# Two stages of a graph network on one core: own tiles, earlier loads and another order at the seam between the stages

## The chip, the core and the metric

The kernel runs on one core of a Trainium2 chip: TensorE (PE) for matmuls, with its weight loads shown apart (PEld), VectorE (DVE), ScalarE (ACT), GpSimd (POOL), and SyncE (SP), which here only issues DMAs. The engines work side by side and hand over by semaphores. The metric is the device time in microseconds (us); lower is better. The kernel before takes 1154.79 us (median of 3 runs, 1154.49 to 1154.93).

## What is computed

3125 nodes with 256 features, 53125 edges sorted by target node. Cut to what matters (`seg` is the segment sum over target nodes):

```
n   = seg(w * x[src])                                   # stage 1
o   = leaky(x @ W1.T + b1 + (n + n*x) @ W2.T + b2)
x1  = layernorm(x + o / |o|)
e   = relu(edge_attr @ ee_w1 + ee_b1) @ ee_w2 + ee_b2   # edge network
h   = (1+eps)*x1 + seg(x1[src] + e)                     # stage 2
h   = relu(ln(h @ w1 + b1)); h = relu(ln(h @ w2 + b2))  # 256 -> 1024 -> 1024
y   = relu(ln(x1 + h @ w3 + b3))
out = layernorm(x1 + y)
```

## The kernel before

Nodes are tiled in 25 blocks of 128 rows, edges in 17 tiles of 128 per block (the last block, number 24, has 8). Every fp32 operand of a large product is split in a high part (rounded to the PE's fast format) and a low part (the rest), and the products high-high, high-low and low-high are summed in PSUM.

**Stage 1**, blocks 0 to 24. POOL gathers the 17 tiles `raw` of source rows, ACT and DVE make from them the messages `msg` (high, low), DVE makes one-hot matrices `oh` from the targets, PE sums messages per target (`ps_sum`, `near_step`), and also runs the edge network's first layer (`ps_e`). A block's tail follows one and two blocks later, interleaved: `take_s` (DVE, makes `s_r` from the sum and the node rows `xs`), `turn` (PE transposes), `turned` (ACT, `sT`), `products` (PE, into `ps_d` and, for the edge part, `ps_w` or `ps_e`), `leak`, `norm`, `deviation`, `table_high` (ACT), and eleven DVE steps `tail(b, 1)` to `tail(b, 11)`: step 1 makes `o`, 4 reads the node rows again (`xr`), 6 aggregates the statistics, 8 makes x1, 9 makes `tb`, 10 the low half of the block's `table` (x1 plus the edge bias, in two halves), 11 makes `hb`. SP stores `table`, x1 and `hb` to HBM (`store_table`, `put_table`, `store_hb`). `table`, `x1` and `hb` have two tiles each, used in turn, so `hb` of block 24 may only be written when the store of `hb` of block 22 has landed. Block 24 already has its own tile for x1 and table.

**Stage 2**, 25 iterations p: first block 24 (p = 0), then block 0, 1, ... . POOL gathers `table` rows from HBM into `grow` (256 KB a tile), PE sums them by one-hots into `ps_s`, DVE makes `h` (`take_h`), PE transposes it (`turn_h`), ACT and DVE split it (`h_high`, `h_low`), then come `layer1`, `layer2`, `layer3` on PE with `stats`, `scalars`, `normalize` (`zn`), PE transposes (`turn_z`), `relu` on ACT and `split` on DVE between them. From p = 2 on the iterations run in one steady order; p = 0 and p = 1 (`first_block`, `late_iteration`) are written apart.

**The seam.** Rows of the last four blocks are not in HBM when the first gathers of stage 2 run. So the early gathers fetch zero rows for them, and `add_absent` adds their share by PE from count matrices `counts` and the table tiles on chip. Block 21's table tile has been reused by then: SP loads it back from HBM (`far_row`). The weights of stage 2 (`w_raw`) are split at the seam too: ACT makes the high parts (`weight_highs(first, end)`, one 128x1024 instruction per piece, 12 pieces), PE copies a high half into a PSUM bank (`copy_highs`, a matmul with the identity `ident_r`), DVE subtracts it from the raw weights (`first_lows`, `weight_lows_from_copies`). Semaphores `w_high`, `w_copied`, `w_ready` count these; `half_bank(m)` says which PSUM bank copy m uses, and `half_bank_free(m)` how many lows must be done before.

The order of the work is written out by hand in each engine's program: an instruction waits until its semaphores stand, and everything behind it on its engine waits with it. SP issues its DMAs in program order as well.

## Time and profile before

| | |
|---|---|
| median of 3 runs | 1154.79 us |
| the profiled execution | 1154.48 us, its span 1152.7 us |
| granted clock of PE over the span | 0.990 |
| stage 1, a block | about 21.3 us |
| PE busy | 95% of the span |
| DVE / ACT / POOL busy | 85% / 58% / 69% |

The page of the profile gives busy shares, 40 slices of the span and the costliest groups. The seam lies at about 526 to 590 us. There the timeline of each engine (start, duration, line, operation, what was written from what, and in brackets the idle time before it with what ended it) and tables by stretches of time are the views to read. Matmul durations in the timeline contain a pipeline latency; the distance between starts is the pace.

### The profile page before, as it was taken

How to read it: one execution, taken by the hardware profiler on the slowest of the kernel's cores; microseconds unless marked ns; L12 is line 12 of the kernel's file. 1: busy time of each engine (PE TensorE's matmuls, PEld its weight loads, DVE VectorE, ACT ScalarE, POOL GpSimd, SP SyncE). 2: the span in 40 equal slices, each digit the busy share in tenths (PEclk: the TensorE clock that was granted, in tenths of full speed). 3: DMA queues.
4: the chain of work that ended last, by engine and by line, in shares of the span. 5: the costliest groups of instructions: out<-in, count | busy, mean ns of one | idle time of the engine just before them, and what ended most of it. 6: DMA issues, size and time to landing. Idle time of an engine off the chain costs nothing.

```text
span 1152.7 us, 21077 instructions
## 1 busy us (share of the span) xinstructions
PE 1095.8 (95%) x5335; PEld 905.8 (79%) x5335; DVE 975.2 (85%) x2792; ACT 663.5 (58%) x1600; POOL 800.0 (69%) x840
## 2 busy tenths in 40 slices
PE   6899999999999999998789999999999999999996
PEld 4688778787787787776578888888888888888885
DVE  7899999999999999998688778877887788778865
ACT  4576777776767776666434454445444544454453
POOL 7777777777777777777567767767776777677610
PEclk9899999999999999999899999999999999999999
DMA  8457667677676566668767777777777777777720
GB/s 228 135 159 202 196 198 209 190 202 207 185 207 182 167 177 178 175 175 267 215 186 221 217 204 215 216 207 211 208 216 207 211 208 215 208 210 208 205 72 12
DMA packets 105664, 222.26 MB, mean 193 GB/s; under 512 B 19959, under 2 KB 56689, under 8 KB 105586
## 3 DMA queue, kind: packets, MB, share of 16 engines
q0 software_dynamic: 53408, 164.16, 50.9%
q1 hardware_dynamic: 52178, 57.25, 16.1%
q8 instruction: 27, 0.44, 0.2%
q14 instruction: 51, 0.42, 0.1%
HBM read 203.97 MB, written 17.36 MB: 192 GB/s over the span
## 4 chain that ended last, share of the span: by engine, by line
PE 52%; POOL 20%; issue 16%; DVE 6%; DMA 4%; ACT 1%; POOLq 0%; SPq 0%; DVEq 0%; ACTq 0%
PE ps_z L1251 29%; POOL raw L873 20%; PE ps_s L1206 9%; PE ps_y L1251 6%; PE ps_tr L1320 3%; DMA raw<-in_x,src_all 3%; DVE oh L158 1%; DVE msg L1966 1%; DVE msg L1972 1%; DMA hbase_dram<-hb 1%; PE ps_e L1005 1%; POOL raw L858 1%; DMA xr<-in_x 1%; PE ps_tr L1245 1%; PE ps_sum L1010 0%
## 5 line engine op out<-in xcount | busy, mean ns | idle before, releaser
L928 POOL DMA_INDIRECT grow<-table_dram,src_all x401 | 386.3, 963 | 166.0 <-issue 96.9
L873 POOL DMA_INDIRECT raw<-in_x,src_all x399 | 378.9, 950 | 121.6 <-issue 113.0
L1251 PE MATMUL ps_z<-w_high,a 128*128 128x512 f32 x784 | 252.9, 394 | 0.5 <-DVE a L2296 0.5
L1005 PE MATMUL ps_e<-we,attr 65*128 65x256 f32 x832 | 224.8, 391 | 15.7 <-DVE msg L1972 13.5
L158 DVE TENSOR_SCALAR oh<-lane,rel 128x128 fp32r<-128x128 f32 x919 | 221.1, 300 | 18.3 <-DMA raw<-in_x,src_all 18.2
L1010 PE MATMUL ps_sum<-msg,oh 128*128 128x512 f32 x464 | 227.6, 491 | 7.3 <-DVE msg L1972 7.3
L1524 ACT ACTIVATE msg<-raw,w_sb 128x256 fp32r<-128x256 f32 x416 | 193.9, 500 | 64.3 <-DMA raw<-in_x,src_all 54.2
L1005 PEld LDWEIGHTS ps_e<-we,attr 65*128 65x128 f32 x832 | 154.0, 194 | 55.0 <-issue 32.3
L1966 DVE SCALAR_TENSOR_TENSOR msg<-raw,w_sb,msg 128x256 fp32r<-128x256 f32 x416 | 181.7, 473 | 6.6 <-ACT msg L1527 6.6
L1012 PE MATMUL ps_sum<-msg,oh 128*128 128x512 f32 x464 | 183.9, 396 | 0.0
L1251 PEld LDWEIGHTS ps_z<-w_high,a 128*128 128x128 f32 x784 | 147.3, 188 | 30.8 <-issue 0.9
L1707 ACT ACTIVATE aF<-ps_tr,be,g 128x128 f32<-128x128 f32 x392 | 144.2, 464 | 37.9 <-PE ps_tr L1320 37.9
L1251 PE MATMUL ps_z<-w_low,a 128*128 128x512 f32 x392 | 152.9, 390 | 0.0
L1972 DVE SCALAR_TENSOR_TENSOR msg<-ps_e,msg 128x512 fp32r<-128x512 f32 (+1 forms) x220 | 142.6, 648 | 0.0
L1527 ACT ACTIVATE msg<-ps_e 128x512 fp32r<-128x512 f32 (+1 forms) x220 | 122.5, 557 | 14.3 <-PE ps_e L1005 14.1
L1206 PE MATMUL ps_s<-grow,oh 128*128 128x512 f32 x455 | 120.1, 400 | 2.4 <-DVE oh L158 2.4
L1010 PEld LDWEIGHTS ps_sum<-msg,oh 128*128 128x128 f32 x464 | 88.3, 190 | 32.1 <-issue 15.8
L2251 DVE BATCH_NORM_STATS2 bs<-ps_z 128x6 f32<-128x512 f32 x100 | 69.6, 697 | 44.7 <-PE ps_z L1251 44.6
L1012 PEld LDWEIGHTS ps_sum<-msg,oh 128*128 128x128 f32 x464 | 88.9, 192 | 15.7
L1206 PEld LDWEIGHTS ps_s<-grow,oh 128*128 128x128 f32 x455 | 83.6, 188 | 18.8 <-DVE oh L158 3.2
L1713 ACT ACTIVATE fm<-fm,ln_eps 128x1 f32<-128x1 f32 x50 | 14.7, 295 | 129.7 <-DVE fm L2256 129.7
L1251 PE MATMUL ps_y<-w_high,a 128*128 128x256 f32 x400 | 83.4, 292 | 2.5 <-DVE a L2309 2.1
(168 smaller groups left out, 1500.5 us busy)
## 6 DMA issues: line engine op xcount, KB each, us to landing
attr<-in_attrT SPq DMA_DIRECT2D x50, 192.0 KB, 4.5
raw<-in_x,src_all POOLq DMA_INDIRECT x416, 3.0
grow<-table_dram,src_all POOLq DMA_INDIRECT x401, 3.7
table_dram<-table SPq DMA_DIRECT2D x24, 256.0 KB, 2.8
w_raw<-in_m_w SPq DMA_DIRECT2D x48, 128.0 KB
attr<-in_attrT SPq DMA_DIRECT2D x24, 160.0 KB, 4.2
xs<-in_x SPq DMA_DIRECT2D x25, 128.0 KB
xTb<-in_xT SPq DMA_DIRECT2D x25, 128.0 KB
```

What stands on the lines that cost most here:

```text
L158: ins = dve.tensor_scalar(out_[:, i, :], lanes, which[:, i:i + 1], None, ALU.is_equal)
L873: pool.indirect_dma_start(out=raw[:, j, :], out_offset=None, in_=x, in_offset=bass.IndirectOffsetOnAxis(ap=src_all[:, q * TILES + j:q * TI ...
L928: pool.indirect_dma_start(out=grow[:, j, :].bitcast(F32), out_offset=None, in_=table_dram, in_offset=bass.IndirectOffsetOnAxis(ap=src_all[ ...
L1005: mm = pe.matmul(ps_e[k % 3][:, (j - j0) * D:(j - j0 + 1) * D], attr[:, j * P:(j + 1) * P], we1[:, :], start=True, stop=True)
L1010: pe.matmul(ps_sum[bank][:, :], oh[:, slot, :], msg[:, j, 0, :], start=start, stop=False, skip_group_check=True)
L1012: return pe.matmul(ps_sum[bank][:, :], oh[:, slot, :], msg[:, j, 1, :], start=False, stop=stop, skip_group_check=True)
L1206: return pe.matmul(ps_s[:, :], oh[:, slot, :], grow[:, j, :], start=start, stop=stop, skip_group_check=True)
L1251: mm = pe.matmul(acc, left[a], right[b], start=False, stop=stop and a == 1, skip_group_check=True)
L1524: act.activation(msg[:, j, 0, 0:D], raw[:, j, :], ACT.Copy, scale=w_sb[:, tile_cols(n, j)])
L1707: ins = act.activation(aF[layer][:, k, :], ps_tr[:, half, c * P:(c + 1) * P], ACT.Relu, bias=bb[:, k:k + 1], scale=gg[:, k:k + 1])
L1966: dve.scalar_tensor_tensor(msg[:, j, 1, 0:D], raw[:, j, :], w_sb[:, tile_cols(n, j)], msg[:, j, 0, 0:D].bitcast(F32), ALU.mult, ALU.subtract)
L1972: dve.scalar_tensor_tensor(msg[:, j0:j0 + m, 1, D:2 * D], ps_e[k % 3][:, 0:m * D].rearrange("p (j d) -> p j d", d=D), 0.0, msg[:, j0:j0 + ...
```

## The change

- `own_table`: block 23 gets an own table tile too, so block 21's stays on chip in `table[1]`, and the load of `far_row` goes.
- `hb` of block 24 is written to a free tile (`raw[:, 1, :]`), is not stored to HBM, and its wait on the store of block 22 goes.
- The last rows of x (`xs`, `xT` of block 24, `xr` of block 23) go to free `raw` tiles and are loaded in the middle of block 23, `res` already in block 15.
- The first bias (512 KB) has its own tile and is loaded in block 21 in four parts, the scales `g`, `be` in block 22; `bng`, `bnb` (128 KB each) are loaded after the last stores.
- The one-hots of block 24's steps 2 and 3 are made by ACT, inside block 23 (`last_one_hots`: per step two squares of 128x128 and one relu of 128x256), no longer by DVE.
- Tails of the last three blocks on DVE, `weight_highs` on ACT, `copy_highs` and the sums of p = 1 on PE are reordered; copies 12 to 19 use four banks, not two.

```diff
             def table_at(b, par):
-                return last_table if is_last(b) else table[par]
+                return own_table[b] if isinstance(b, int) and b in own_table else table[par]
+            def hb_at(b, par):
+                return raw[:, 1, :] if is_last(b) else hb[par]
...
-            last_table = w3_high[:, 1:3, :]
-            far_row = w3_high[:, 3:5, :].rearrange("p a d -> p (a d)")
+            own_table = {BLOCKS - 1: w3_high[:, 1:3, :], BLOCKS - 2: w3_high[:, 3:5, :]}
...
             def half_bank(m):
...
-                return (ps_y[:, :], ps_z[1][:, 1, :] if m < FIRST_HALVES else ps_tr[:, 1, :])[m % 2]
+                if m < FIRST_HALVES:
+                    return (ps_y[:, :], ps_z[1][:, 1, :])[m % 2]
+                return (ps_z[0][:, 0, :], ps_z[0][:, 1, :], ps_y[:, :], ps_tr[:, 1, :])[(m - FIRST_HALVES) % 4]
...
             def half_bank_free(m):
...
-                return 5 if m == 8 else m - 1
+                if m < FIRST_HALVES:
+                    return 5 if m == 8 else m - 1
+                if m < FIRST_HALVES + 4:
+                    return FIRST_HALVES - 1 if m == FIRST_HALVES + 2 else 0
+                return m - 3
...
             def load_weight_part(b, part):
...
+                if b == FIRST_COUNT + TILES + 2:
+                    sp.wait_ge(counted, TILES)
+                    sp.dma_start(bias_0[:, cols], m_b1[:, cols]).then_inc(bias_in[0], 16)
...
                 for b in range(1, BLOCKS - 1):
...
                    load_xT(b)
                    load_weight_part(b, 2)
+                    if b == BLOCKS - 2:
+                        sp.wait_ge(message, NP * b + 6)
+                        sp.dma_start(xT_at(b + 1), xT[:, :, bass.ds((b + 1) * P, P)]).then_inc(late_xT_in, 16)
+                        sp.dma_start(xs_at(b + 1), rows(x, b + 1)).then_inc(late_xs_in, 16)
+                        sp.dma_start(xr_at(b), rows(x, b)).then_inc(late_xr_in[0], 16)
...
-                sp.dma_start(res[:, :], rows(x, BLOCKS - 1)).then_inc(xr_last_in, 16)
-                load_xs(BLOCKS - 1)
-                load_xT(BLOCKS - 1)
-                load_xr(BLOCKS - 2)
-                sp.wait_ge(counted, TILES)
-                load_consts()
-                sp.wait_ge(message, NP * (BLOCKS - 1) + LAST_PAIRS)
-                sp.wait_ge(table_stored, 16 * (BLOCKS - ABSENT_BLOCKS + 1))
-                sp.dma_start(far_row.bitcast(F32), rows(table_dram, BLOCKS - ABSENT_BLOCKS)).then_inc(row_in, 16)
-                load_bias(0)
                 store_table(BLOCKS - 3, 0)
                 store_hb(BLOCKS - 3, 0)
                 store_table(BLOCKS - 2, 1)
                 put_table(BLOCKS - 1, 0)
                 load_bias(1)
                 store_hb(BLOCKS - 2, 1)
-                store_hb(BLOCKS - 1, 0)
+                load_norms()
...
+            def last_one_hots(path, c):
+                last, n = BLOCKS - 1, c - LAST_OH
+                span, j0, m = path.steps[c]
+                lanes = lane[:, (1 - span) * P:(2 - span) * P]
+                wait(act, last_oh, n)
+                for j in range(m):
+                    at = last * TILES + j0 + j
+                    act.activation(sq[:, j * P:(j + 1) * P], lanes, ACT.Square, bias=rel_columns[:, at:at + 1],
+                                   scale=-1.0).then_inc(last_squared, 1)
+                act.wait_ge(last_squared, m * (n + 1))
+                act.wait_ge(summed, SUMS * (last - 1) + c + 1)
+                act.activation(oh[:, path.slot[c]:path.slot[c] + m, :].rearrange("p j n -> p (j n)"), sq[:, 0:m * P],
+                               ACT.Relu, bias=ones_c[:, :], scale=-1.0).then_inc(last_oh, 1)
...
                 def first_block():
-                    h_high(0)
-                    act.wait_ge(bias_in[0], 16)
+                    act.wait_ge(bias_in[0], 64)
                     act.wait_ge(w_ready, 1)
                     open_z(0, 0, 0)
                     act.wait_ge(w_ready, 2)
                     open_z(0, 0, 1)
-                    weight_highs(5, 8)
+                    h_high(0)
+                    weight_highs(4, KD + KH - 2)
...
                 def first_block(path):
...
                     add_absent(1)
-                    sums(path, 1, 1, SPLIT_SUM)
-                    copy_highs(FIRST_HALVES, FIRST_HALVES + 2)
+                    sums(path, 1, 1, 2)
+                    copy_highs(FIRST_HALVES, FIRST_HALVES + 4)
                     layer2_with(0, 0, w2_high, 0, KH // 2)
-                    copy_highs(FIRST_HALVES + 2, FIRST_HALVES + 3)
+                    copy_highs(FIRST_HALVES + 4, FIRST_HALVES + 5)
                     layer2_with(0, 0, w2_high, KH // 2, KH)
-                    copy_highs(FIRST_HALVES + 3, FIRST_HALVES + 4)
+                    copy_highs(FIRST_HALVES + 5, FIRST_HALVES + 6)
+                    sums(path, 1, 2, LAST_PAIRS)
```

DVE at the end of stage 1 and the start of stage 2, before: `hb` of block 24 (which waits for a store), four one-hots, then `h` (p = 0).

```order
L2140 TENSOR_TENSOR w_low<-w_raw,ps_z 128x512 [waits w_copied]
L2030 TENSOR_TENSOR w_high<-tb,w_high 128x256 [waits da_end2]
L2036 SCALAR_TENSOR_TENSOR hb<-raw,eps_t,ps_e 128x256 [waits hb_stored,edge_dense,dd_end2]
L158 TENSOR_SCALAR oh<-lane,rel 128x128 [waits sum_done]
L158 TENSOR_SCALAR oh<-lane,rel 128x128 x3
L2238 TENSOR_TENSOR h<-ps_s,hb 128x256 [waits dd_end2,absent_added,sum_done]
```

The same place of DVE now.

```order
L2197 TENSOR_TENSOR w_low<-w_raw,ps_z 128x512 [waits w_copied]
L2086 TENSOR_TENSOR w_high<-tb,w_high 128x256 [waits da_end2]
L2093 SCALAR_TENSOR_TENSOR raw<-raw,eps_t,ps_e 128x256 [waits edge_dense,dd_end2]
L2197 TENSOR_TENSOR w_low<-w_raw,ps_z 128x512 [waits w_copied]
L2294 TENSOR_TENSOR h<-ps_s,raw 128x256 [waits dd_end2,absent_added,sum_done]
```

The wait `hb_stored` is gone, the second weight low stands behind `hb`, and the four one-hots have moved behind the first `stats` of p = 0.

ACT from the message of block 24's tiles 6 and 7 to x1's deviation of block 23, before (`sT` are the transposes of block 23, then of block 24).

```order
L1623 ACTIVATE ident_r<-ident 128x128 [waits counted]
L1534 ACTIVATE sT<-ps_t 128x512 [waits edge_dense,s_turned]
L1516 ACTIVATE w_high<-w_raw 128x1024 [waits edge_net,w_in]
L1551 ACTIVATE st<-st,ln_eps 128x1 [waits dd_end0]
L1539 ACTIVATE ol<-ps_d 128x256 [waits dd_end0,dense]
L1545 ACTIVATE sq,st<-o 128x256 [waits dd_end1]
L1547 ACTIVATE st<-st 128x1 [waits da_end1]
L1555 ACTIVATE table<-tb 128x256 [waits dd_end0]
L1516 ACTIVATE w_high<-w_raw 128x1024
L1534 ACTIVATE sT<-ps_t 128x512 [waits edge_dense,s_turned]
```

And now.

```order
L1677 ACTIVATE ident_r<-ident 128x128 [waits message]
L1570 ACTIVATE sT<-ps_t 128x512 [waits edge_dense,s_turned]
L1552 ACTIVATE w_high<-w_raw 128x1024 [waits edge_net,w_in]
L1552 ACTIVATE w_high<-w_raw 128x1024
L1587 ACTIVATE st<-st,ln_eps 128x1 [waits dd_end0]
L1575 ACTIVATE ol<-ps_d 128x256 [waits dd_end0,dense]
L1581 ACTIVATE sq,st<-o 128x256 [waits dd_end1]
L1583 ACTIVATE st<-st 128x1 [waits da_end1]
L1570 ACTIVATE sT<-ps_t 128x512 [waits edge_dense,s_turned]
L1591 ACTIVATE table<-tb 128x256 [waits dd_end0]
```

Both first weight highs stand ahead of block 23's `leak` (`ol`), and block 24's `sT` ahead of block 22's `table` high.

PE around the start of the second layer of p = 0, before (`a` is the split result of the first layer; the copies are those from the identity).

```order
L1206 MATMUL ps_s<-grow,oh 128x512 [waits got4,oh2_ready]
L1206 MATMUL ps_s<-grow,oh 128x512 [waits got5]
L1193 MATMUL ps_y<-w_high,ident_r 128x512 [waits w_ready,w_high]
L1193 MATMUL ps_tr<-w_high,ident_r 128x512 [waits relu_out0,w_ready,w_high]
L1287 MATMUL ps_z<-w_high,a 128x512 [waits a_ready0,z_open1_0]
L1287 MATMUL ps_z<-w_high,a 128x512 x7
L1193 MATMUL ps_y<-w_high,ident_r 128x512 [waits w_ready,w_high]
L1287 MATMUL ps_z<-w_high,a 128x512 [waits a_ready0]
L1287 MATMUL ps_z<-w_high,a 128x512 x7
L1193 MATMUL ps_tr<-w_high,ident_r 128x512 [waits w_ready,w_high]
```

And now.

```order
L1230 MATMUL ps_z<-w_high,ident_r 128x512 [waits w_high] x2
L1230 MATMUL ps_y<-w_high,ident_r 128x512 [waits w_ready,w_high]
L1230 MATMUL ps_tr<-w_high,ident_r 128x512 [waits relu_out0,w_high]
L1324 MATMUL ps_z<-w_high,a 128x512 [waits a_ready0,z_open1_0]
L1324 MATMUL ps_z<-w_high,a 128x512 x7
L1230 MATMUL ps_z<-w_high,ident_r 128x512 [waits w_ready,w_high]
L1324 MATMUL ps_z<-w_high,a 128x512 [waits a_ready0]
L1324 MATMUL ps_z<-w_high,a 128x512 x7
L1230 MATMUL ps_z<-w_high,ident_r 128x512 [waits w_ready,w_high]
L1243 MATMUL ps_s<-grow,oh 128x512 [waits got4,oh2_ready]
```

The second layer now starts behind step 1 of p = 1 and four copies, not behind steps 1 and 2 and two copies, and the sums 2 and 3 stand later.

## Rows read from the trace of the kernel before

**Rows 1.** The page, part 1: busy time and share of the span.

```profile
PE 1095.8 (95%) x5335; PEld 905.8 (79%) x5335; DVE 975.2 (85%) x2792; ACT 663.5 (58%) x1600; POOL 800.0 (69%) x840
```

**Rows 2.** Table by stretches: length, busy (instructions) by engine, clock, DMA share, GB/s.

```profile
540.00:560.00 20.00, 13.83 (x62) 10.49 (x60) 12.88 (x33) 9.77 (x18) 10.49 (x12) 0.83 0.90 314
600.00:620.00 20.00, 20.00 (x96) 16.56 (x95) 14.37 (x48) 6.24 (x17) 15.12 (x17) 1.00 0.76 226
```

**Rows 3.** Timeline of PE at the seam: start, duration, what, idle before it.

```profile
551.53 1.22 PE L1193 MATMUL ps_z<-w_high,ident_r 128*128 128x512 f32 x2 [4.18 <-DVE hb L2036]
...
568.94 0.73 PE L1206 MATMUL ps_s<-grow,oh 128*128 128x512 f32 x2 [2.14 <-DVE oh L158]
...
569.97 3.38 PE L1287 MATMUL ps_z<-w_high,a 128*128 128x512 f32 x8
...
573.57 2.07 PE L1287 MATMUL ps_z<-w_high,a 128*128 128x512 f32 x8
...
581.05 0.40 PE L1251 MATMUL ps_z<-w_high,a 128*128 128x512 f32 x1
...
590.68 1.07 PE L1320 MATMUL ps_tr<-ident,zn 128*128 128x128 f32 x8
```

**Rows 4.** Timeline of DVE at the seam.

```profile
551.00 0.48 DVE L2036 SCALAR_TENSOR_TENSOR hb<-raw,eps_t,ps_e 128x256 f32<-128x256 f32 x1 [4.21 <-DMA hbase_dram<-hb]
551.39 0.87 DVE L158 TENSOR_SCALAR oh<-lane,rel 128x128 fp32r<-128x128 f32 x4
552.18 0.42 DVE L2238 TENSOR_TENSOR h<-ps_s,hb 128x256 f32<-128x256 f32 x1
552.51 0.68 DVE L2214 TENSOR_TENSOR w_low<-w_raw,ps_z 128x512 fp32r<-128x512 f32 x1
...
560.31 0.81 DVE L2276 TENSOR_SCALAR zn<-ps_z,mv 128x512 f32<-128x512 f32 x1
...
567.94 1.06 DVE L158 TENSOR_SCALAR oh<-lane,rel 128x128 fp32r<-128x128 f32 x5
...
579.12 0.42 DVE L2240 TENSOR_TENSOR h<-ps_s,hbx 128x256 f32<-128x256 f32 x1 [1.37 <-PE ps_s L1206]
...
587.41 1.28 DVE L2251 BATCH_NORM_STATS2 bs<-ps_z 128x6 f32<-128x512 f32 x2
```

**Rows 5.** The chain that ended last: start, duration, what.

```profile
540.42 10.45 DMA hbase_dram<-hb
```

**Rows 6.** Timeline of SP at the seam.

```profile
536.62 0.43 SPq L707 DMA_DIRECT2D bias<-in_m_b  x1
...
537.63 0.34 SPq L665 DMA_DIRECT2D table_dram<-table  x1
...
550.71 0.38 SPq L665 DMA_DIRECT2D table_dram<-w_high  x1
```

**Rows 7.** Waits of SP, 500 to 600 us: total, times, longest.

```profile
SPq L657 <- DMA table_dram<-table: 7.5, 1, 7.5
```

**Rows 8.** Groups by line and form, ACT: busy, mean ns.

```profile
L1516 ACT ACTIVATE w_high<-w_raw 128x1024 fp32r<-128x1024 f32 x12 | 12.2, 1052 | 0.0
...
L1575 ACT ACTIVATE squares<-lane,rel 128x128 f32<-128x128 f32 x17 | 6.7, 395 | 0.0
```

**Rows 9.** Table by stretches, PE only: busy (instructions), clock, DMA share, GB/s.

```profile
550.00:551.00 1.00, 0.00 (x0) 0.50 0.40 151
556.00:557.00 1.00, 1.00 (x5) 0.70 0.76 201
```

**Rows 10.** The same table as rows 9, in stage 1.

```profile
130.00:151.00 21.00, 20.18 (x94) 1.00 0.70 199
469.00:490.00 21.00, 20.18 (x90) 1.00 0.62 176
```

**Rows 11.** Timeline of POOL at the seam.

```profile
553.72 0.94 POOL L928 DMA_INDIRECT grow<-table_dram,src_all  x1 [6.47 <-DMA table_dram<-w_high]
```

**Rows 12.** The page, part 6: a DMA issue, count, KB, median us to landing.

```profile
table_dram<-table SPq DMA_DIRECT2D x24, 256.0 KB, 2.8
```

167 lines of the change are left out of this document (96 added, 71 removed).

## The prediction

> **What bounds the kernel now.** I read the page first, then a table by stretches, then the timelines of PE, DVE, ACT, SP and POOL at the seam, and last the chain that ended last. PE is busy for 1095.8 of 1152.7 us [rows 1]. In the steady part of stage 2 it is busy 20.00 of 20 us; at the seam 13.83 of 20 us, at a mean granted clock of 0.83 [rows 2]. So stage 2 is bound by PE, and whatever brings PE earlier into its steady order is gained in full; the change can pay only at the seam. PE's timeline there shows the holes: 4.18 us before 551.53 that DVE's `hb` ended, 2.14 us before 568.94 that a one-hot ended, and between them the first layer-2 half of p = 0 at 569.97 took 3.38 us where the same 8 matmuls took 2.07 us at 573.57 [rows 3]. The next iteration's layer 2 begins at 581.05, and the transposes that need `zn` of iteration 1 at 590.68 [rows 3]. DVE's timeline names the cause of the first hole: `hb` of block 24 at 551.00 after 4.21 us idle, ended by the store of `hb` of block 22 [rows 4]; the chain shows that store from 540.42 on, 10.45 us [rows 5].
>
> Why it takes so long: SP had just issued four loads of rows, four small ones, `bng`, `bnb`, `far_row` and, at 536.62, a 512 KB bias, then at 537.63 the store of block 22's table [rows 6], whose landing SP itself awaited for 7.5 us [rows 7]. The table of block 24 was issued at 550.71 only [rows 6].
>
> **The change part by part.** I carry each engine's order of the changed kernel forward by the durations of the rows, from 529 us on; up to there I expect nothing.
>
> *Term 1, up to `h` of p = 0 (DVE, 552.18 before).* The wait of 4.21 us goes, since the new tile waits for no store. The four one-hots between `hb` and `h`, 551.39 to 552.18, move behind `h`: 0.8 us. The loads of `xs`, `xT`, `xr` are issued in block 23, some 12 us earlier; the idle 0.55 us of DVE for `xs` at 536.47, 1.35 us of PE for `xT` and 0.85 us of DVE for `xr` go, and DVE is rid of the last four one-hots of stage 1, another 0.8 us. Against that, two weight highs, not one, now stand on ACT ahead of block 23's `leak`; one costs 1.05 us, so 0.95 us later by start to start [rows 8]; and one weight low (0.68 us long, 0.6 in a row [rows 4]) stands where DVE was idle before. Of about 2.2 us gained and 1.5 us lost here I keep 0.6. Sum 5.6 us: `h` at about 546.6. Bounds: 4.2 us (inputs help nothing) to 6.5 us (the highs find a gap).
>
> *Term 2, from `h` to the start of layer 2 (552.18 to 569.97 before, 17.8 us).* PE's granted clock was 0.50 at 550 to 551 and only back within 556 to 557 [rows 9]: it fell inside the hole before 551.53, so the 12 matmuls of layer 1 ran at 1.2 GHz. Without that hole I expect 2.4 GHz, and DVE's idle time for `stats`, about 1.9 us, goes; the moved one-hots come in, 0.8 us. From `zn` (560.31) on, DVE's list is the same work with one more low in it, 0.6 us, which stood before it earlier. So the splits of p = 0 end about 14.8 us after `h`, before 15.8. And layer 2 starts with the first half of the split, not after the one-hots that ended at 569.0 (five, 1.06 us at 567.94 [rows 4]), two sums and two copies: that is 1.0 us before the end of the splits, where it was 2.0 us behind it. Term 2: 1.0 + 3.0 = 4.0 us. Layer 2 at about 560.4, 9.6 us sooner.
>
> *Term 3, from there to iteration 1 (569.97 to 581.05 before, 11.1 us).* 48 matmuls and sums at 0.23 us are left, at full clock, plus one wait of about 0.9 us for the low of copy 12, which now stands behind the one-hots: 8.8 us. Gain 2.3 us, of which 1.3 is the clock (3.38 against 2.07 us [rows 3]), the rest the 1.4 us that the copies waited in turn on two banks, now four. PE would be 11.9 us sooner at this point.
>
> *Term 4, given back.* DVE gets `h` of p = 1 at about 569.3, against 579.12, 9.9 us sooner; behind it stand the same lows, two direct lows and one-hots before `stats` at 587.41 [rows 4]. From there to ACT's `zn` is 3.13 us, and PE's transposes at 590.68 had 0.14 us of slack. DVE comes 10 us sooner, PE 11.9: PE waits the difference here. This is the new late one. The gain at 590 is 10.0 us, and in the steady order PE is the bound again.
>
> *Costed at nothing.* Block 24's one-hots on ACT: two squares of 0.395 us [rows 8] and a relu, 1.15 us a step by start to start, 2.3 us in block 23. They lie in ACT's idle time before block 21's `tb` (1.95 us) and ahead of message 2, which DVE wants 0.7 us later than it would now be ready. If that cover is gone it costs up to 1 us. The 512 KB of bias in block 21, with 128 KB of `res` in block 15: blocks with 512 KB of weight loads (130 to 151) and without (469 to 490) have the same 20.18 us of PE in 21 [rows 10], so nothing; the queue of SP sees 0.43 us per issue between attribute loads that wait for PE anyway. The three loads in block 23 stand ahead of block 21's store, which waits for DVE until 527.95. POOL's list is unchanged; its first gather of p = 1 waits for block 24's table, at 553.72 before [rows 11]. I expect the table stored from about 545.6 on, and the gather at 548.4; the first four tiles are wanted at 558.8 and land by 557.
>
> For what the stores will take the trace bounds it by 10.45 us [rows 5] and by the 2.8 us that a table store takes in the median [rows 12]; I take 4 us, nearer to the low end, because 5.9 MB are asked of the queues in the 23 us from 526 on, 256 GB/s, where 540 to 560 shows 314 GB/s as its mean [rows 2].
>
> The Trainium skill's page DMA: Bandwidth & Descriptors, section Queues, rings and completion order, says that one issuer's descriptors are consumed in ring order while an engine takes turns between rows. By that rule the store was late mainly because of the 1.5 MB which SP itself had put ahead of it, not because of POOL's gathers, and the late store would vanish with those loads; by a shared limit alone it would shrink less. The 7.5 us which SP waited fits both, and no row here separates them.
>
> The sum: 5.6 + 4.0 + 2.3 - 1.9 = 10.0 us. I take off 0.5 us for some ten handovers between engines which I chained without any slack (estimate, 0.05 us each, as between `hb` and its release). The profiled execution took 1154.48 us, its span 1152.7; the median of the runs is 0.3 us above it. 1154.5 - 9.5 = 1145.0 us.
>
> **The rivals.**
>
> *A, the clock or a hole stays.* PE is still sparse from 543 to 560 by my schedule, somewhat over half busy, with holes of 1 to 2 us. If the clock falls once more, as it did between 568.94 and 573.57 after a hole of 2.14 us, that costs 1.3 to 2.7 us: 1146.5 to 1148. For it: that very fall. Against: 536 to 540 was as sparse, with 1.35 us of hole, and kept its clock.
>
> *B, the stores stay slow.* If block 24's table still goes out at 550.7, the tiles of p = 1 land 3.3 us after they are wanted, and layer 2 shifts by as much: 1148.3. For it: the DMA engines are 0.90 busy in 540 to 560 [rows 2], and the gathers, most of that, remain. Against: a quarter of the bytes of that stretch are gone.
>
> *C, only the wait goes.* If the reordered tails and highs do nothing, 4.2 us of `hb`, 0.8 us of one-hots and the clock at 2.7 us are left, minus 1 us given back: about 6.7 us, 1147.8; 1150 if the clock stays as well.
>
> *D, slower.* One mechanism: PE's clock falls before `h` and stays at 1.2 GHz until layer 2 of p = 1, because the change spreads PE's work more thinly (copies one by one, each behind a low of DVE). From copy 4 to there some 76 matmuls of 128x512 would take 0.2 us more each, 15 us, against 10 gained: 1159.6. It decides from about 50 slow matmuls on. Against: before, the clock came back after 5 us of work which was no denser.
>
> *E, the tiles don't free anything*, because another wait of the same kind (x1 of block 23 on the store of block 21) ends as late: same as before. Against: that x1 came at 540.46 with no idle time.
>
> **How the numbers follow.** My forecast, 1143 to 1146.5: 0.54. A 0.2, B 0.09, C 0.09, D 0.03, E 0.02, faster than 1143 (term 4 is not taken, up to 12 us gained, or 6.5 in term 1) 0.03. The range 1141.8 to 1149.5 leaves out D, E, the worse end of C and some of the unforeseen. 0.2% is 2.3 us, about what a measurement of this kernel can tell from no change: faster 0.95, same 0.02, slower 0.03.
>
> **What would show it.** Right: no idle time on DVE before `hb` of block 24, `h` of p = 0 near 546.6, the granted clock at 1.00 from 546 to 557, layer 2 of p = 0 near 560.4, iteration 1's layer 2 near 569, the table of block 24 issued before 547, and a wait of PE of about 1.5 us at the transposes near 579 to 581. Wrong: a clock of 0.50 anywhere from 546 to 580 (A, D), POOL's first gather of p = 1 later than 551 (B), `leak` of block 23 on ACT over 1 us later than before (C), or more than 0.5 us idle on DVE in block 23 before the messages (the one-hots on ACT are not covered).

## The result

The changed kernel takes 1145.99 us (median of 6 runs, 1145.09 to 1147.71) against 1154.84 us of the kernel before (median of 6, 1154.37 to 1155.55) in the same comparison: ratio 0.9926, 95% interval 0.9916 to 0.9937, so 8.9 us less. Predicted were 1145.0 us, 1141.8 to 1149.5. The profiled execution took 1146.01 us, its span is 1144.2 us, its mean granted clock 0.992. Medians here and below are of all executions of a kernel, ratios of the undisturbed (fast) ones only, so the two need not divide evenly (in e9 above all).

### The profile after

The page, part 1, which answers to [rows 1]: PE has the same work in 8.5 us less span.

```profile
PE 1094.9 (96%) x5335; PEld 905.1 (79%) x5335; DVE 974.2 (85%) x2788; ACT 666.5 (58%) x1606; POOL 799.4 (70%) x840
```

The table by stretches, columns as in [rows 2]: PE is busy for 16.46 us of the seam's 20, not 13.83, but at the same mean clock of 0.83. The stretch from 600 on, which was full, now has a hole of 0.28 us.

```profile
540.00:560.00 20.00, 16.46 (x71) 12.20 (x70) 17.10 (x47) 15.27 (x28) 10.68 (x11) 0.83 0.85 270
600.00:620.00 20.00, 19.72 (x106) 16.55 (x105) 14.24 (x38) 10.25 (x25) 15.13 (x17) 1.00 0.75 218
```

DVE's timeline, which answers to [rows 4]: `hb` of block 24 (now written to `raw`) has no idle time, and `h` of p = 0 comes at 545.98. `stats` still waits 0.70 us for PE.

```profile
544.99 0.47 DVE L2093 SCALAR_TENSOR_TENSOR raw<-raw,eps_t,ps_e 128x256 f32<-128x256 f32 x1
545.98 0.41 DVE L2294 TENSOR_TENSOR h<-ps_s,raw 128x256 f32<-128x256 f32 x1
550.51 0.70 DVE L2307 BATCH_NORM_STATS2 bs<-ps_z 128x6 f32<-128x512 f32 x1 [0.70 <-PE ps_z L1288]
570.64 0.42 DVE L2296 TENSOR_TENSOR h<-ps_s,hbx 128x256 f32<-128x256 f32 x1 [3.96 <-PE ps_s L1243]
```

PE's timeline, which answers to [rows 3]: the copies no longer stand behind a hole of 4.18 us but of 1.50 us, layer 2 of p = 0 begins at 562.55, that of p = 1 at 570.44, and the transposes of p = 1 now wait 1.51 us for `zn`. At 612.06 PE waits for a gathered tile.

```profile
545.13 0.50 PE L1217 MATMUL ps_s<-w_high,counts 128*128 128x256 f32 x2 [1.50 <-DVE w_high L2086]
546.45 0.69 PE L1282 MATMUL ps_tr<-ident,h 128*128 128x128 f32 x2 [0.20 <-DVE h L2294]
...
554.78 1.07 PE L1357 MATMUL ps_tr<-ident,zn 128*128 128x128 f32 x8 [1.36 <-ACT zn L1748]
557.37 2.07 PE L1243 MATMUL ps_s<-grow,oh 128*128 128x512 f32 x4 [0.19 <-DVE oh L159]
562.55 1.97 PE L1324 MATMUL ps_z<-w_high,a 128*128 128x512 f32 x8
570.44 0.39 PE L1288 MATMUL ps_z<-w_high,a 128*128 128x512 f32 x1
581.85 1.07 PE L1357 MATMUL ps_tr<-ident,zn 128*128 128x128 f32 x8 [1.51 <-ACT zn L1748]
612.06 0.50 PE L1243 MATMUL ps_s<-grow,oh 128*128 128x512 f32 x1 [0.24 <-DMA grow<-table_dram,src_all]
```

The same stretches for PE alone (busy, clock, DMA share, GB/s), as [rows 9]: the clock fell twice. The four sums at 557.37, for example, took 2.07 us; e6 below, whose clock was up there, took 1.19.

```profile
546.00:550.00 4.00, 3.68 (x11) 0.57 0.89 266
550.00:556.00 6.00, 4.60 (x25) 1.00 0.80 269
556.00:560.00 4.00, 3.68 (x8) 0.57 0.82 241
560.00:576.00 16.00, 16.00 (x71) 1.00 0.76 224
```

SP's and POOL's timelines, which answer to [rows 6, 11]: block 24's table goes out at 546.37, not at 550.71, and yet POOL's first gather of p = 1, which waits for it, starts at the same time as before.

```profile
538.97 0.33 SPq L700 DMA_DIRECT2D table_dram<-table  x1
...
546.37 0.41 SPq L700 DMA_DIRECT2D table_dram<-w_high  x1
```

```profile
553.75 0.94 POOL L963 DMA_INDIRECT grow<-table_dram,src_all  x1 [6.29 <-DMA table_dram<-w_high]
```

The DMA view (KB each, us from issue to landing) of block 22's table store, first in the kernel before (issued at 537.63 [rows 6]), then in the changed one (538.97):

```profile
table_dram<-table SPq DMA_DIRECT2D x1, 256.0 KB, 10.6
```

```profile
table_dram<-table SPq DMA_DIRECT2D x1, 256.0 KB, 3.7
```

I follow the lead over the kernel before at PE's transposes of `h`, one per iteration: 6.20 us at p = 0 (552.65 to 546.45), 10.63 at p = 1, 8.76 at p = 2, 8.20 at p = 3, and from there to the end a slow rise to 8.62. So the seam decides, and what the lead is at p = 3 is what the kernel gains. The table shows it for all profiled executions that can be compared.

| kernel | p = 0 | 1 | 2 | 3 | median us | ratio to before (95%) |
|---|---|---|---|---|---|---|
| changed | 6.20 | 10.63 | 8.76 | 8.20 | 1145.99 | 0.9926 (0.9916 to 0.9937) |
| e1, own `hb` tile alone | 4.70 | 6.03 | 4.52 | 4.52 | 1150.05 | 0.9967 (0.9954 to 0.9980) |
| e2, `hb` wait back | 5.35 | 9.49 | 7.60 | 7.61 | 1146.65 | 0.9936 (0.9922 to 0.9950) |
| e3, holes filled | 6.19 | 12.18 | 10.55 | 8.87 | 1144.24 | 0.9913 (0.9898 to 0.9928) |
| e4, fillers in the kernel before | -1.75 | -0.45 | -0.44 | -0.43 | 1154.26 | 0.9998 (0.9989 to 1.0007) |
| e5, one-hots on DVE | 6.21 | 10.52 | 8.76 | 8.78 | 1145.92 | 0.9931 (0.9917 to 0.9945) |
| e6, old PE order | 5.55 | 7.64 | 6.12 | 6.12 | 1148.38 | 0.9952 (0.9938 to 0.9966) |
| e7, old ACT order | 5.56 | 9.50 | 6.32 | 6.34 | 1146.23 | 0.9925 (0.9913 to 0.9938) |
| e8, loads late | 2.00 | 7.95 | 6.17 | 6.17 | 1147.33 | 0.9934 (0.9920 to 0.9948) |

The kernel before took 1153.89 us beside e1 to e4 and 1154.99 us beside e5 to e8, so medians of different groups compare only roughly. By the ratios e6 is 3.0 us slower than the changed kernel (2.4 by the medians), e2 1.2, e8 0.9, e5 0.6, e7 0.1 faster and e3 1.5 faster; of these only e6 has an interval that does not overlap that of the changed kernel.

A profiled execution is one of a kernel's runs; where it is not near the median (e7: 1147.64 us, the longest of its six) its leads say how that one went, not what the edit costs. It can also come to the seam late for a reason that lies long before it: DVE's `o` of block 22 stands at 528.10 in the changed kernel and within 0.12 us of it in e1, e2, e3 and e5, but at 528.29 in e7, 528.67 in e8 and 528.76 in e6, and e6 was 0.67 us behind at 121 us already. So 0.66 us of e6's smaller lead, 0.57 of e8's and 0.19 of e7's are not their edits'. And in e1, e6 and e7 the clock fell once more, within 588 to 596 (third layer of p = 1; 0.68 in e6 and 0.57 in e7 at 588 to 592, 0.74 in e1 at 592 to 596), behind the usual waits for `zn`. I read the loss of 1.5 us from p = 1 to p = 2 in e1 and e6, and part of the 3.2 in e7, as that.

### The profile page after: what moved, and what is told of

Read it like the earlier page. It is cut to its first block, busy times and chain, and to the rows that moved or that the text cites. A ratio compares the mean times of both kernels' runs of the same rounds, so it can differ in the third digit from the quotient of the medians.

```text
span 1144.2 us, 21077 instructions
## 1 busy us (share of the span) xinstructions
PE 1094.9 (96%) x5335; PEld 905.1 (79%) x5335; DVE 974.2 (85%) x2788; ACT 666.5 (58%) x1606; POOL 799.4 (70%) x840
## 4 chain that ended last, share of the span: by engine, by line
PE 51%; POOL 20%; issue 17%; DVE 7%; DMA 3%; ACT 1%; SPq 1%; POOLq 0%; DVEq 0%; ACTq 0%
PE ps_z L1288 27%; POOL raw L908 19%; PE ps_s L1243 8%; PE ps_y L1288 6%; PE ps_tr L1357 3%; DMA raw<-in_x,src_all 2%; DVE oh L159 2%; DVE msg L2020 1%; DVE msg L2026 1%; PE ps_e L1040 1%; POOL grow L963 1%; PE ps_sum L1045 1%; PE ps_sum L1047 1%; DMA attr<-in_attrT 1%; PE ps_tr L1282 0%
```

## The experiments

### e1: the own tile of `hb` alone

The kernel before with one part of the change: block 24's `hb` in `raw[:, 1, :]`, not stored, no wait.

```diff
+            def hb_at(b, par):
+                return raw[:, 1, :] if is_last(b) else hb[par]
...
-                    wait(dve, hb_stored, 16 * (b - lag))
+                    if not is_last(b):
+                        wait(dve, hb_stored, 16 * (b - lag))
```

> The kernel before with one edit: hb of block 24 has its own tile, is not stored, and waits for no store. Theory 1 (the wait was one of several causes, and the clock another): hb at about 546.8 us, h of p = 0 at 548, 4.2 us sooner; POOL's first gather of p = 1 still near 553.7, so step 1 of p = 1 waits a little for its tiles; PE's clock still falls once or twice. Time about 1150, 4 to 5.5 us under before. Rival (the wait alone is the gain of the change): 1146 to 1147, within 1 us of the changed kernel.

Measured: 1150.05 us, ratio 0.9967; lead 4.70 us at p = 0 and 4.52 at the end. Theory 1 holds, the rival (the wait alone is the whole gain) falls. The clock stayed up where it had been 0.50 [rows 9], and fell later, at 562 to 568, behind PE's wait of 2.00 us for a one-hot:

```profile
546.00:550.00 4.00, 2.58 (x11) 1.00 0.96 347
550.00:556.00 6.00, 4.66 (x24) 1.00 0.88 266
556.00:562.00 6.00, 4.74 (x20) 1.00 0.79 216
562.00:568.00 6.00, 5.05 (x15) 0.72 0.69 206
```

So the wait of 4.21 us [rows 4] is worth about half of the whole gain, and the clock that it had cost was mostly paid again a little later.

### e2: the wait back in the changed kernel

```diff
             def hb_at(b, par):
-                return raw[:, 1, :] if is_last(b) else hb[par]
+                return hb[par]
...
-                    if not is_last(b):
-                        wait(dve, hb_stored, 16 * (b - lag))
+                    wait(dve, hb_stored, 16 * (b - lag))
```

> The changed kernel, but hb of block 24 is written to the shared tile again and waits for the store of block 22. It tells what made that store slow. Theory 1 (the loads which SP had put ahead of it): the store is issued near 541.3 and lands after some 6 us, so DVE idles about 2 us before hb (not 4.2), and the time is 1147 to 1148.5. Rival (the early gathers alone keep the DMA engines full, the store takes 10 us as before): DVE idles 6 us before hb, near 551.5, and the time is 1151 to 1152.

Measured: 1146.65 us, ratio 0.9936; its interval overlaps that of the changed kernel. DVE's timeline shows the wait, 0.56 us, where theory 1 expected some 2 us and a time of at least 1147:

```profile
545.74 0.48 DVE L2092 SCALAR_TENSOR_TENSOR hb<-raw,eps_t,ps_e 128x256 f32<-128x256 f32 x1 [0.56 <-DMA hbase_dram<-hb]
```

The store was issued at 541.30 and landed 4.4 us later, where it had taken 10.45 us [rows 5]. The rival (still 10 us) falls. The two parts are alternatives: with the loads out of SP's way the new tile saves 0.6 us of waiting, without that 4.2. The Trainium skill's page DMA: Bandwidth & Descriptors, section Queues, rings and completion order, has one issuer's descriptors consumed in ring order on each DMA engine, and the prediction drew from it that the late store would vanish with the 1.5 MB ahead of it; by this rule, the run agrees, with 4.4 for 10.45 us. But it does not single the rule out. The same 1.5 MB are gone from all that is in flight too, and a limit shared by all queues would also make the store faster; how much, no run here shows.

### e3 and e4: work for PE in its holes

Matmuls of 128x512 that nobody reads, into free PSUM banks. In e3 six of them stand in the changed kernel ahead of the last counts (the hole of 1.50 us), five ahead of the transposes at 554.78, two behind a copy, ahead of sums that wait for a one-hot; in e4 seven and seventeen in the two holes of the kernel before.

```diff
+                def fill(bank, m):
+                    for _ in range(m):
+                        pe.matmul(bank, ident_r[:, :], flat(pieces[0][1], 0), start=True, stop=True,
+                                  skip_group_check=True)
...
+                        if p == 0 and n == ABSENT_BLOCKS - 1:
+                            pe.wait_ge(dd_end[-1], 1)
+                            fill(ps_tr[:, 1, :], 6)
```

> The changed kernel with matmuls on PE whose results nobody reads, in the two holes in which its granted clock fell: 6 of 128x512 ahead of block 24's share in the sum of p = 0, 5 ahead of the transposes of the first layer of p = 0, 2 behind copy 10. Theory 1 (what is missing to the forecast is PE's clock at 1.2 GHz from 546 to 550 and from 557 to 560): the clock stays at 1.00 through 546 to 561, layer 2 of p = 0 starts near 560.5 and not 562.5, and the time is 1143.5 to 1144.5. Rival (the clock is off the path, DVE sets the pace there): the clock stays up and the time is the same, 1145.7 to 1146.3; with the fillers in the way, 1146.5.

Measured: 1144.24 us, ratio 0.9913, the fastest kernel here, though its interval overlaps that of the changed one. Theory 1 holds in the trace, the rival (the clock is off the path) does not. The clock stayed up through the seam:

```profile
546.00:550.00 4.00, 3.29 (x15) 1.00 0.98 317
550.00:556.00 6.00, 5.60 (x27) 1.00 0.95 313
556.00:560.00 4.00, 3.99 (x17) 1.00 0.79 226
560.00:576.00 16.00, 15.60 (x69) 1.00 0.74 218
```

PE's timeline has the schedule of the prediction: layer 2 at 560.49 (predicted 560.4), the transposes of p = 1 waiting 1.35 us (1.5), and, behind it, waits for gathered tiles.

```profile
560.49 1.98 PE L1333 MATMUL ps_z<-w_high,a 128*128 128x512 f32 x8
...
580.15 1.06 PE L1366 MATMUL ps_tr<-ident,zn 128*128 128x128 f32 x8 [1.35 <-ACT zn L1759]
...
610.21 0.47 PE L1252 MATMUL ps_s<-grow,oh 128*128 128x512 f32 x1 [0.88 <-DMA grow<-table_dram,src_all]
611.39 0.50 PE L1252 MATMUL ps_s<-grow,oh 128*128 128x512 f32 x1 [0.28 <-DMA grow<-table_dram,src_all]
```

The lead of 10.55 us at p = 2 fell to 8.87 at p = 3. Against e3 the changed kernel is 2.06 us late at layer 2 of p = 0 (562.55 against 560.49), 1.55 at that of p = 1, 1.79 at p = 2: the price of its two falls of the clock. At p = 3 it is 0.67: the kernel that comes sooner loses more to the wait for tiles.

> The kernel before with such matmuls in its hole: 7 ahead of block 24's share, 17 more while PE waits for hb of block 24. It prices the first fall of the clock by itself. Theory 1: the clock stays at 1.00 from 546 to 560, layer 1 of p = 0 takes 2.7 us and not 4, DVE's stats come 1.5 to 2 us sooner, the time is 1152.7 to 1153.5. Rival (DVE has enough other work at that place): the clock stays up, the time is within 0.5 us of before.

Measured: 1154.26 us, ratio 0.9998 (0.9989 to 1.0007). This prices nothing: the clock had fallen ahead of the first fillers (0.60 at 544 to 546), and the seventeen ran on past the `h` for which the hole waited, so PE's transposes of it came at 554.40 instead of 552.65. The filler was too large for the hole it was to fill.

### e5: the last one-hots back on DVE

```diff
-                    if b == BLOCKS - 2 and s in (6, 8):
-                        last_one_hots(path, LAST_OH if s == 6 else LAST_OH + 1)
...
                 take_s(before, SUMS * last, 1)
+                near_oh(path, last, 2)
+                near_oh(path, last, 3)
                 messages(2)
```

> The changed kernel (0.9926 of before, 1145.99 us), with one thing undone: the one-hots of block 24's steps 2 and 3 are made by DVE again, behind the first two messages' place, not by ACT inside block 23. Theory 1 (they were on DVE's path at the end of stage 1, four of 128x128, 0.8 us together): hb of block 24 and h of p = 0 come 0.8 us later (h at about 546.8 instead of 545.98), and the time is 1146.4 to 1146.8 us at the same before, 0.4 to 0.8 more than the changed kernel. Rival (ACT's one-hots only fill a gap which DVE had too, because DVE waits for PE or POOL there): h within 0.2 us of 545.98 and the time within 0.3 us of the changed kernel.

Measured: 1145.92 us, ratio 0.9931, and `h` of p = 0 at 545.97, where the changed kernel has 545.98:

```profile
545.97 0.41 DVE L2290 TENSOR_TENSOR h<-ps_s,raw 128x256 f32<-128x256 f32 x1
```

This execution came to the seam 0.12 us ahead (`o` of block 22 at 527.98), so the four one-hots cost 0.11 us of the 0.8 that theory 1 gave them; the rest is covered by waits of DVE that were there anyway. Theory 1 falls, the rival holds: to move them to ACT brought next to nothing. The run shows something else. SP issued block 24's table at 545.14, 1.23 us sooner, since its own wait for earlier stores was shorter; it landed in 5.4 us, POOL's gathers began at 551.31, and the lead stayed at 8.78 us from p = 2 to 3, where the changed kernel lost 0.56 us. POOL also stood still once, which it did not in the changed kernel:

```profile
551.31 0.98 POOL L963 DMA_INDIRECT grow<-table_dram,src_all  x1 [4.18 <-DMA table_dram<-w_high]
...
568.32 0.95 POOL L963 DMA_INDIRECT grow<-table_dram,src_all  x1 [0.72 <-PE ps_s L1240]
```

### e6: PE's order and banks undone

Copies 12 to 19 on two banks, sums 2 and 3 of p = 1 ahead of the first half of layer 2, ACT's openings of `ps_z` in the old place.

```diff
-                    sums(path, 1, 1, 2)
-                    copy_highs(FIRST_HALVES, FIRST_HALVES + 4)
+                    sums(path, 1, 1, SPLIT_SUM)
+                    copy_highs(FIRST_HALVES, FIRST_HALVES + 2)
```

> The changed kernel with PE's order around layer 2 of p = 0 undone: copies 12 to 19 use two banks again, the sums 2 and 3 of p = 1 stand ahead of the first half, and ACT opens ps_z of the next layer in its old order. Tiles, loads and one-hots stay as changed. Theory 1 (my terms 2 and 3: layer 2 starts 3.0 us sooner relative to DVE's splits, the two banks cost 1.4 us): layer 2 of p = 0 starts at about 565 instead of 562.55, iteration 1's layer 2 at 572.5 to 573.5 instead of 570.44; but the changed kernel gave 1.9 us of PE's lead back to DVE at the transposes near 581.85, so only what exceeds 1.9 us reaches the end, less the second fall of the clock that may go with denser work: 1146.3 to 1147.5 us. Rival (the order costs nothing, since DVE sets the pace up to the transposes at 581.85): h of p = 1 and the transposes at the same times as in the changed kernel, time within 0.3 us of it.

Measured: 1148.38 us, ratio 0.9952, whose interval lies just above that of the changed kernel: 2.4 us more by the medians, and more than the 1147.5 us that theory 1 allowed. PE waits again for the one-hots, starts layer 2 at 564.01 and p = 1 at 573.40, and the transposes of p = 1 wait for nothing:

```profile
562.97 0.73 PE L1237 MATMUL ps_s<-grow,oh 128*128 128x512 f32 x2 [2.66 <-DVE oh L159]
564.01 1.98 PE L1318 MATMUL ps_z<-w_high,a 128*128 128x512 f32 x8
...
573.40 0.39 PE L1282 MATMUL ps_z<-w_high,a 128*128 128x512 f32 x1
...
583.08 1.06 PE L1351 MATMUL ps_tr<-ident,zn 128*128 128x128 f32 x8
```

The clock stayed at 1.00 from 546 to 576, so this execution is best compared with e3, whose clock did too. From PE's transposes of `h` of p = 0 to layer 2 of p = 1, e3 needs 22.4 us (546.46 to 568.89), e6 26.3 us (547.10 to 573.40): the order is worth 3.9 us there. To the transposes of p = 1 e3 needs 33.7 us, e6 36.0: 2.3 us are left, the rest is given back. The medians of e6 and of the changed kernel differ by 2.4, but the clock fell in other places in the two, so that this is nearly the same number proves little. Theory 1 holds for the places and the direction, the rival falls.

### e7: ACT's order of the weight highs undone

```diff
-                weight_highs(0, 2)
+                weight_highs(0, 1)
...
+                weight_highs(1, 2)
                 turned(last)
```

> The changed kernel with ACT's order of weight_highs undone: one high, not two, ahead of block 23's leak, one behind block 23's table high, and in stage 2 the highs 5 to 8 in one piece behind the openings of ps_z. Theory 1 (moving them makes the early copies and lows ready sooner, and the last lows do not wait for ACT behind h): hb of block 24 comes up to 0.9 us sooner since leak is not delayed, but the highs behind h are late and DVE or PE waits for w_ready after it: together 1145.8 to 1147.5 us. Rival (the two highs ahead of leak are a pure delay of 0.95 us and the rest is covered): hb at 544.0 to 544.4 instead of 544.99, and 1145.0 to 1145.5 us.

Measured: 1146.23 us, ratio 0.9925: no difference by the medians. But its profiled execution has `hb` of block 24 at 545.63, 0.64 us later than the changed kernel, not sooner; it was 0.16 us behind before (`o` of block 23 at 535.49, not 535.33), so the edit's share is about 0.5. ACT's timelines say why, first that of e7, then that of the changed kernel:

```profile
535.01 0.38 ACT L1575 ACTIVATE ol<-ps_d 128x256 f32<-128x256 f32 x1 [0.81 <-PE ps_d L1109]
...
537.25 1.04 ACT L1552 ACTIVATE w_high<-w_raw 128x1024 fp32r<-128x1024 f32 x1
538.20 0.58 ACT L1570 ACTIVATE sT<-ps_t 128x512 f32<-128x512 f32 x1
```

```profile
532.62 2.00 ACT L1552 ACTIVATE w_high<-w_raw 128x1024 fp32r<-128x1024 f32 x2
534.84 0.38 ACT L1575 ACTIVATE ol<-ps_d 128x256 f32<-128x256 f32 x1
...
537.53 0.60 ACT L1570 ACTIVATE sT<-ps_t 128x512 f32<-128x512 f32 x1 [1.00 <-PE ps_t L1075]
```

With one high ahead of `leak` (`ol`), ACT waits 0.81 us for `ps_d`; the second high fits there. In its old place it stands ahead of block 24's `sT`, which is on the path. Both theories had the sign of this wrong: two highs ahead of `leak` delay nothing.

### e8: the loads back at their old time

```diff
-                if n == N_SPLIT and part == 0:
-                    sp.dma_start(res[:, :], rows(x, BLOCKS - 1)).then_inc(late_xr_in[1], 16)
...
+                last = BLOCKS - 1
+                sp.dma_start(res[:, :], rows(x, last)).then_inc(late_xr_in[1], 16)
+                sp.wait_ge(s_ready, last)
+                sp.dma_start(xs_at(last), rows(x, last)).then_inc(late_xs_in, 16)
...
+                for part in range(4):
+                    cols = slice(part * 256, (part + 1) * 256)
+                    sp.dma_start(bias_0[:, cols], m_b1[:, cols]).then_inc(bias_in[0], 16)
                 store_table(BLOCKS - 3, 0)
```

> The changed kernel with the loads issued late again: res, xs, xT of block 24, xr of block 23, the four scales and the first bias (512 KB, in four parts) are issued behind block 23, ahead of block 22's stores, as before; their own tiles stay, far_row stays away, bng and bnb stay behind the last stores. So 1.0 to 1.2 MB stand again ahead of the stores on SP. Theory 1 (the stores were late by what SP itself had put ahead of them, and DVE and PE waited for xs, xT, xr): DVE waits 0.5 us for xs and 0.8 for xr again, hb of block 24 near 546.3, table of block 24 stored later, POOL's first gather of p = 1 near 555 instead of 553.75, time 1147.2 to 1148.5 us. Rival (the gathers' bytes alone make the loads and stores slow, their order on SP does not matter): hb within 0.3 us of 544.99, the gather near 553.75, time within 0.4 us of the changed kernel. Since only hb's wait for the store was removed by the new tile, a store of block 22's hb that takes about 10 us again shows theory 1, one of about 4.4 us the rival.

Measured: 1147.33 us, ratio 0.9934, 1.3 us more by the medians with overlapping intervals. The wait came back larger than theory 1 had it (3.42 us, not 0.5), and on the load, not on the store:

```profile
537.66 0.42 DVE L2040 SCALAR_TENSOR_TENSOR s_r<-raw,ps_sum 128x256 f32<-128x256 f32 x1 [3.42 <-DMA raw<-in_x]
```

`xs` landed 7.1 us after its issue; block 22's table, made late and so issued at 542.21, then landed in 4.5 us. `hb` of block 24 came at 549.19 (theory 1: 546.3), POOL's first gather of p = 1 at 553.16, nearer to the rival's 553.75 than to theory 1's 555. So theory 1 has the direction and the time right and the place wrong: the loads asked of the queues within 529 to 534 took 6.2 to 7.1 us. The sign that was to decide between the two, how long the store of block 22's `hb` takes, can't be read, because nothing waits for that store any more; and the 4.5 us of block 22's table decide nothing, since it went out 3.2 us later than in the changed kernel, when SP's loads ahead of it were mostly done (estimate: the four parts of the bias, issued from 536.20 on, took 6.9 us in the median). Whether SP's own order or the sum of all bytes makes a store slow stays open.

The lead at p = 0 fell by 4.2 us, of which 0.57 was lost ahead of the seam, at p = 3 by 2.0 us only; this execution's clock fell at 540 to 546 and not later, so part of what it lost stood in place of the changed kernel's two falls.

### e9 to e12: four kernels on a chip that can't resolve them

e9 stores block 23's table without waiting for the stores before it, e10 does so on top of e3, e11 also sends the second bias behind the landing of block 24's table, e12 is e4 with 5 and 9 matmuls.

```diff
-                store_table(BLOCKS - 2, 1)
+                put_table(BLOCKS - 2, 1)
                 put_table(BLOCKS - 1, 0)
-                load_bias(1)
                 store_hb(BLOCKS - 2, 1)
+                sp.wait_ge(table_stored, 16 * BLOCKS)
+                load_bias(1)
                 load_norms()
```

> The changed kernel (0.9926 of before) with one edit: the store of block 23's table no longer waits until the stores of the earlier blocks' tables and x1 have landed (SP waited 2.7 + 2.7 us there; the tiles are block 23's own, nothing needs that order). So block 23's table goes out near 543 instead of 545.46, block 24's near 545.2 instead of 546.37, and POOL's first gather of p = 1, which waits for its landing, comes near 551 instead of 553.75. Theory 2 (the late gathers cost about 0.5 us between p = 2 and p = 3, as the kernel with DVE's one-hots, whose gathers began at 551.31, kept its lead of 8.8 us where the changed kernel fell from 8.76 to 8.20): lead over before at the fourth iteration 8.7 to 8.8 us and 0.3 to 0.6 us less time than the changed kernel, ratio about 0.9921. Rival (PE does not need the gathers so soon; the 0.5 us have another cause): lead 8.2 and no difference. A third (the stores side by side only slow each other): the gather not before 553.

> The same edit on top of the kernel with 6 + 5 + 2 unread matmuls in PE's holes (which took 1144.24 us; its lead over before was 10.55 us at p = 2 and 8.87 at p = 3, gathers from 551.59 on, PE waiting 0.88 and 0.28 us for gathered tiles at 610 to 611). Theory 2 (POOL's chain of gathers, 1.25 us each without a pause from 551.59 on, is what PE runs into; each us by which it starts sooner is a us gained up to the 10.5 us lead): gathers from about 550.7 on, lead 9.5 to 10 us at p = 3, time 1143.2 to 1143.8 us, ratio 0.9905. Rival (PE's waits there come from the bandwidth, not from POOL's start): lead stays near 8.9, time 1144.2 us.

> As the kernel before in this list, and also the second bias (512 KB), the two scales bng, bnb and the third bias are issued only when block 24's table has landed, behind the store of block 23's hb. Theory 2: the table lands 1 to 1.7 us sooner still (512 KB less beside it at about 300 GB/s), gathers of p = 1 from about 549.5 on, lead 10 to 10.5 us at p = 3, time 1142.5 to 1143.3 us, unless ACT now waits for the second bias, which it wants at about 556. Rival (the table's landing is set by the gathers ahead of it, and the bias behind it does not matter, as ring order would have it): first gather within 0.4 us of the kernel with the unwaited store, same time, or slower by what ACT waits for the bias.

> The kernel before with unread matmuls of 128x512 in PE's two holes at 545 and 547.5 to 551.5, 5 and 9 of them (7 and 17 overran the hole at the low clock). All waits of the kernel stay, so this asks what the clock alone is worth. Theory 1 (the fall of the clock inside the hole cost DVE 1.9 us of waiting for stats, of which most comes back later because iteration 1 has another wait, 2.14 us for one-hots): granted clock 1.00 from 546 to 556, h of p = 0 unchanged near 552, lead over before 1 to 2 us at p = 1, 0.5 to 1.5 us less time: ratio 0.9987 to 0.9996. Rival (DVE's list sets the pace behind h, and the slow matmuls of layer 1 are hidden beside it): no difference, 0.9998 to 1.0003. If the clock falls earlier all the same, the run settles nothing.

Measured: the chip that ran these took 1537.16 us for the kernel before (35 runs, 1517.61 to 1579.67), a third more than the others. e9: 1540.84, ratio 0.9906 (0.9848 to 0.9965); e10: 1531.11, 0.9898 (0.9849 to 0.9947); e11: 1531.76, 0.9939 (0.9892 to 0.9986); e12: 1535.37, 1.001 (0.9959 to 1.006). PE stood still there again and again without a wait that the profile shows, as in e9:

```profile
780.54 0.49 PE L1288 MATMUL ps_z<-w_high,a 128*128 128x512 f32 x1 [1.03 <-issue]
781.97 0.39 PE L1288 MATMUL ps_z<-w_high,a 128*128 128x512 f32 x1 [0.94 <-issue]
783.38 0.58 PE L1288 MATMUL ps_z<-w_low,a 128*128 128x512 f32 x1 [1.03 <-issue]
```

The intervals are 0.9 to 1.2% wide, where differences of 0.05 to 0.2% were asked for, so none of the theories of these four is settled, and whether e10 beats e3 is open. One reading stands without the times: block 24's table went from issue to the first gather in 2.8 us in e9 (722.08 to 724.90), in e10 (719.66 to 722.48) and in e11 (722.97 to 725.78), with the bias of 512 KB right behind it or not. There the gathers ahead of it had long landed. In the changed kernel the same store takes 6.6 us. That fits with the traffic ahead of the store, and not the bias behind it, as what makes it slow, but where everything else is stretched as well it doesn't show it.

## Why the prediction was right

The time is 1.0 us above the forecast and inside its range, even inside the narrower 1143 to 1146.5, although the clock fell twice, which the prediction had kept for rival A. So the mechanism was right in the main, and part of the number is luck. Step by step:

**Term 1, -5.6 us, measured -6.2.** `h` at 545.98 against 546.6. The wait is gone, `hb` also comes 1.8 us sooner than its old ready time (551.00 less 4.21 is 546.79, now 544.99), the one-hots behind it are gone (0.8), a low stands between (0.6). The term was 0.6 us too small because I took 0.95 us off for the second high ahead of `leak`; e7 shows that it fits in a gap and spares about 0.5 us at `sT` instead. That the one-hots of steps 2 and 3 gave 0.8 us was wrong (0.11, e5).

**Term 2, layer 2 at 560.4, measured 562.55.** The step that failed is "the granted clock at 1.00 from 546 to 557". It fell twice, at 546 to 550 and 556 to 560: rival A's mechanism, at a chance of 0.2. With the clock up (e3) layer 2 stands at 560.49. The order of work in this term, and in term 3, is worth nearly what was worked out: 4.4 us predicted (3.0 and 1.4), 3.9 measured between e3 and e6 (2.9 and 1.0). One reading was wrong: not all 12 matmuls of layer 1 were slow before. The last six stand at a pace of 0.23 us, from 557.10 on.

**Term 3, 8.8 us from layer 2 to iteration 1, measured 7.9 (562.55 to 570.44).** PE came so late that the low for copy 12, for which a wait of 0.9 us was predicted, was ready. e3, which came in time, has 8.4 us with a wait of 0.40. The count in the sum was a slip: 48 matmuls at 0.23 us would be 11.0 us. There are 34, which is 7.8 us and, with the wait of 0.9, about the 8.8 that the sum used.

**Term 4, 1.9 us given back, measured 1.87** (10.63 to 8.76), with the wait of 1.51 us at the transposes that the prediction named. In e3 it is 1.63, at 1.35 us of wait. The slow clock was not absorbed here: its 1.55 us at layer 2 of p = 1 are still 1.70 at the transposes (581.85 against 580.15), since DVE too had waited for the slow matmuls (0.70 us before `stats`).

Why DVE is the late one here is to be seen in its row at 570.64 above: it stood idle for 3.96 us (3.97 in e3) until PE's last sums of p = 1, which the change put right ahead of layer 2. The 11.2 us from there to the transposes are its list behind `h`: three lows, two direct lows and 13 one-hots, then `stats`. So DVE has not too much work here but too much of it behind `h`; whether some of it could go into the idle time was not tried.

**The stores.** "I take 4 us": 3.7 for block 22's table (10.6 before), 4.4 for its `hb` (e2). For block 24's it was wrong: issued at 546.37, within the predicted time, it took 6.6 us, and the gather came at 553.75 instead of 548.4, "later than 551", the sign of rival B. The other executions with this order of stores took 4.4 to 5.6 us, with the gather at 550.43 (e2) to 551.69 (e7): better, and still not 4 us and 548.4. Nor is a quarter of the bytes gone, as was set against B: 540 to 560 carries 270 GB/s, not 314, a seventh less. But B's price, 3.3 us at layer 2 of p = 1, was not paid: PE waits for no tile ahead of 612.06. A smaller one was paid two iterations later, 0.56 us in the changed kernel and 1.68 in e3, where POOL issues a gather about every 1.25 us without a pause from the first of p = 1 on and so has no slack to catch up.

**C** is right in that the highs bring nothing in time (e7), and its sign, `leak` over 1 us later, did not come (534.84 for 534.03). It falls with e6 and e1: PE's order is worth 2 to 3 us, and with the wait alone the kernel takes 1150.05 us. **D** needed a clock that stays low and some 50 slow matmuls; it was back within 4 us each time. **E** falls: neither x1 of block 23 (539.00) nor `hb` of block 24 has idle time ahead of it.

So the forecast of 9.5 us is made of 0.6 more in term 1, 10.55 us at p = 2 if the clock holds (predicted 10.0), less 1.8 for the clock and 0.56 for the gathers; of these two the sum held nothing, and the 0.5 us taken off for handovers was about as large as the second of them by chance. That the late gathers cause the loss from p = 2 to p = 3 rests on PE's waits at 610 to 612, and on this: the changed kernel and e3 are the two in which POOL never paused for PE from the first gather of p = 1 to 612 us, and the two that lost. In e1, e2 and e5 to e8 it paused once or twice, by 0.7 to 1.9 us, and no lead fell. It is not shown by a run of its own; those that were to test it (e9, e10) don't settle it.

## What to carry to other kernels

When two parts of a change remove the same wait (a free tile, and less traffic ahead of the store that is awaited), each alone gives most of it (all 4.21 us in e1; 0.56 left in e2) and together they give little more: price them as alternatives. Follow each gain to the place where another engine becomes the late one (here DVE, at the transposes of p = 1): only what that engine also gains is kept. Before two profiled executions are compared at the seam, look how far apart they are ahead of it (up to 0.66 us here). And a transfer that is hidden at the iteration that first reads it may still come up two iterations later, where its issuer has no slack to catch up.
